# Rotary attention on one NeuronCore: the inverted softmax sums, split in two parts, are spread over the heads by eight 128-row fp32r products instead of sixteen 32-row fp32 ones

## The reference, cut to what matters

```python
q = layer_norm(layernorm(x)); k = v = layer_norm(ctx)       # x: 2 x 2048 x 512, ctx: 2 x 128 x 512
qh, kh = rope(heads(q @ Wq)), rope(heads(k @ Wk))           # 16 heads of 64
vh = heads(v @ Wv)
aw = 30 * tanh((qh . kh) / 8 / 30); aw = where(pad | causal, -inf, aw)
p = softmax(aw, axis=-1)
out = (p . vh, heads side by side) @ Wo
x = x + out
```

## Time and profile before

| | |
|---|---|
| median of 3 runs | 1569.18 us (1568.81 to 1569.34) |
| span of the profiled execution | 1565.3 us |
| median less span | 3.9 us (no separate time is given for the profiled execution) |
| PE busy, DVE busy | 1471.0 us (94%), 1184.2 us (76%) |
| rotary attention's chunks | about 61 to 645 us of the span |
| from one chunk's `recip` to the next | 36.73 us |

### The profile page before, as it was taken

One profiled execution on the slowest core, in us unless ns is written; L12 is line 12 of the kernel. 1 busy time (PEld: TensorE's weight loads), 2 busy tenths in 40 slices (PEclk: granted clock), 3 DMA queues, 4 the chain that ended last, 5 costly groups with the idle time before them and its releaser, 6 DMA issues. The chain is left out here.

```text
span 1565.3 us, 30701 instructions
## 1 busy us (share of the span) xinstructions
PE 1471.0 (94%) x10998; PEld 1078.9 (69%) x11022; DVE 1184.2 (76%) x2306; ACT 881.9 (56%) x2093; POOL 489.1 (31%) x436
## 2 busy tenths in 40 slices
PE   7899999999999999599998998999999977998997
PEld 5677777777777777444443467888888866776885
DVE  5677777886777655478878968888888756787875
ACT  3444444444444443456657838888988865664342
POOL 0122222222222221200002544545545434664333
PEclk9999999999999999799999999999999998999998
DMA  8411111110111101113304810000000007225641
GB/s 308 153 45 44 44 44 44 44 40 8 43 34 34 43 8 75 44 75 148 148 1 178 324 40 3 4 2 2 3 4 3 4 1 269 82 82 182 205 151 60
DMA packets 47808, 118.35 MB, mean 76 GB/s; under 512 B 9422, under 2 KB 15950, under 8 KB 46032
## 3 DMA queue, kind: packets, MB, share of 16 engines
q1 hardware_dynamic: 42016, 100.03, 18.1%
q0 software_dynamic: 5680, 16.85, 2.7%
HBM read 78.89 MB, written 39.80 MB: 76 GB/s over the span
## 5 line engine op out<-in xcount | busy, mean ns | idle before, releaser
L1721 ACT ACTIVATE c_probs<-c_score,c_minus_top 128x128 f32<-128x128 f32 x512 | 183.8, 422 | 2.0 <-DVE c_minus_top L1833 2.0
L1676 POOL TENSOR_TENSOR c_probs<-c_probs,c_recip 128x1024 f32<-128x1024 f32 x64 | 121.7, 1902 | 169.7 <-DVE c_recip L1839 169.7
L689 POOL TENSOR_TENSOR a_attn_lo_parts<-a_attn,a_attn_hi_parts 128x512 fp32r<-128x512 f32 x64 | 80.1, 1285 | 250.2 <-ACT a_attn_hi_parts L747 250.2
L1721 ACT ACTIVATION_READ_ACCUMULATOR c_probs<-c_score,c_minus_top 128x1 f32 x512 | 133.9, 262 | 0.0
L743 ACT COPY a_attn<-a_pv_ps 128x512 f32<-128x512 f32 x64 | 37.0, 578 | 162.7 <-PE a_pv_ps L998 162.6
L425 PE MATMUL a_bank<-a_x_hi_parts,a_wq_hi 128*128 128x256 f32 x512 | 106.8, 290 | 0.3 <-PEq L440 0.3
L2287 ACT CAST d_xT_hi<-d_turn 128x512 fp32r<-128x512 f32 x71 | 41.7, 587 | 110.1 <-PE d_turn L2531 103.1
L425 PE MATMUL a_bank<-a_x_lo_parts,a_wq_hi 128*128 128x256 f32 x512 | 103.0, 283 | 0.0
L425 PE MATMUL a_bank<-a_x_hi_parts,a_wq_lo 128*128 128x256 f32 x512 | 102.8, 282 | 0.0
L966 PE MATMUL a_bank<-a_wo_hi,a_attn_hi_parts 128*128 128x512 f32 x256 | 102.4, 400 | 0.0
L967 PE MATMUL a_bank<-a_wo_lo,a_attn_hi_parts 128*128 128x512 f32 x256 | 101.1, 395 | 0.0
(11 more groups left out here) (310 smaller groups left out, 4276.0 us busy)
## 6 DMA issues: line engine op xcount, KB each, us to landing
hidden<-b_hidden SPq DMA_DIRECT2D x5, 2816.0 KB, 8.1
b_hidden<-hidden SPq DMA_DIRECT2D x5, 2816.0 KB, 11.9
xres<-in_x SPq DMA_DIRECT2D x8, 1024.0 KB, 14.0
d_we<-in_we SPq DMA_DIRECT2D x8, 1024.0 KB, 12.7
xres<-in_w_gate_up SPq DMA_DIRECT2D x7, 1024.0 KB, 5.3
d_got<-rows SPq DMA_DIRECT2D x20, 258.0 KB, 2.9
xres<-rows SPq DMA_DIRECT2D x19, 258.0 KB, 2.9
a_rot<-in_rot SPq DMA_DIRECT2D x16, 256.0 KB, 3.1
```

The source lines that it names most:

```text
L689: nc.gpsimd.tensor_tensor(of_spread(attn_lo, g), of_spread(attn, g), of_spread(attn_hi, g), ALU.subtract).then_inc(attn_lo_ready, 1)
L1676: nc.gpsimd.tensor_tensor(part, part, recip[:, t % 2, heads].unsqueeze(2).to_broadcast([P, HALF, KEYS]), ALU.mult).then_inc(scaled, 1)
L1721: last = nc.scalar.activation(probs[:, t, at, :], score_ps[:, h, g, :], ACT.Exp, bias=minus_top[:, h, g:g + 1], accum_out=total[:, t, at:a ...
```

## The change

The inverted sums are made in three steps on DVE: `reciprocal` into half of the scratch tile `swapped`, a copy of it rounded to fp32r into the other half, and a `scalar_tensor_tensor` that writes rounded * s + full into the fp32r tile `recip`, where s is 0 on the rows with row % 32 < 16 and -1 on the others. So half of the rows hold the rounded value and the other half the rest. Each step waits for the one before. The products of `spread` now use all 128 rows: one product gives the 128 rows of two heads, with a 0/1 matrix that has two ones in each column (rounded part and rest), 4 products a `spread`, 8 a chunk. That matrix (`pick_heads`, 128x1024) is made once by POOL at the start of the second block; TensorE waits for it once, in chunk 0. To make room, `q` holds two units instead of four and its buffer is used in turn, and `x_full` moves from `q` to the place of `x_lo`.

```diff
-        sum_to, pick = sb("sum_to", [P, 32 + UNITS - 1]), sb("pick", [P, UNITS])
+        sum_to, pick = sb("sum_to", [P, 32 + UNITS - 1]), sb("pick", [P, H0 + 1])
...
-        recip = sb("recip", [P, ROPE_CHUNK])
+        recip = sb("recip", [P, ROPE_CHUNK], F32R)
+        recip_full, recip_hi = swapped[:, 0, :], swapped[:, 1, :].bitcast(F32R)
...
-        q = sb("q", [P, BLOCKS, ROPE_CHUNK])
-
-        x_full = q[:, 0:KB, :]
+        q = sb("q", [P, 2, 2, ROPE_CHUNK])
+        pick_heads = sb("pick_heads", [P, H0, DH0], F32R)
+
+        x_full = nc.alloc_sbuf_tensor_at("a_x_full", [P, KB, ROPE_CHUNK], F32, offset=front_offset + 4 * KB * ROPE_CHUNK)
...
+                nc.gpsimd.tensor_copy(pick_heads[:], pick[:, 0:H0].unsqueeze(2).to_broadcast([P, H0, DH0])).then_inc(pick_ready, 1)
                 chunks(pool, body)
...
-                    nc.vector.tensor_tensor(q[:, 2 * g:2 * g + 2, :], src[:], by_angle(0), ALU.mult)
+                    nc.vector.tensor_tensor(q[:, g % 2], src[:], by_angle(0), ALU.mult)
...
                         dve.wait_ge(summed, UNITS * (n + 1))
-                        nc.vector.reciprocal(recip[:], sum_ps[:, 0, :]).then_inc(recip_ready, 1)
+                        ch.step(nc.vector.reciprocal(recip_full, sum_ps[:, 0, :]))
+                        ch.wait()
+                        ch.step(nc.vector.tensor_copy(recip_hi, recip_full))
+                        ch.wait()
+                        nc.vector.scalar_tensor_tensor(recip[:], recip_hi, pick[:, H0:], recip_full, ALU.mult, ALU.add).then_inc(recip_ready, 1)
...
                         if m == 0:
                             pe.wait_ge(recip_ready, n + 1)
+                            if isinstance(n, int) and n == 0:
+                                pe.wait_ge(pick_ready, 1)
                         out = [begin(f"B{2 * m + i}") for i in range(2)]
                         for i in range(2):
-                            for h in range(4):
-                                rows = slice(32 * h, 32 * (h + 1))
-                                last = nc.tensor.matmul(out[h // 2][h % 2 * DH0:(h % 2 + 1) * DH0, i, :], pick[rows, 2 * m + i:2 * m + i + 1].to_broadcast([32, DH0]), recip[rows, :],
-                                                        start=True, stop=True)
+                            for j in range(2):
+                                heads = slice(H0 // UNITS * (2 * m + i) + 2 * j, H0 // UNITS * (2 * m + i) + 2 * j + 2)
+                                last = nc.tensor.matmul(out[j][:, i, :], pick_heads[:, heads, :].rearrange("p h d -> p (h d)"), recip[:], start=True, stop=True)
                         last.then_inc(bank_full, 2)
...
-        "pick": (at[:, None] % 32 == np.arange(UNITS)[None, :]).astype(np.float32),
+        "pick": np.concatenate([(at[:, None] % 16 == np.repeat(np.arange(UNITS), 4)[None, :]) & (at[:, None] // 32 == np.tile(np.arange(4), UNITS)[None, :]),
+                                -1.0 * (at[:, None] % 32 >= 16)], axis=1).astype(np.float32),
```

More of the change, by code:

```diff
@@ L325, in rope_attention_stage @@
         summed, recip_ready = sem("summed"), sem("recip_ready")
-        dve_step = sem("dve_step")
+        dve_step, pick_ready = sem("dve_step"), sem("pick_ready")
         ld_raw, weight_step, piece_ready, stored, ld_last = (sem(x) for x in ("ld_raw", "weight_step", "piece_ready", "stored", "ld_last_x"))
@@ L615, in rope_attention_stage @@
         assert next_offset(nc) <= ahead.top
-        DVE_STEPS = 2 * NT + UNITS - 1
+        DVE_STEPS = 2 * NT + UNITS - 1 + 2
         score_banks = score_ps[:].rearrange("p u h c -> p (u h c)").bitcast(BF16).rearrange("p (i c) -> p i c", i=4)
@@ L810, in rotate_end @@
                         ch.wait()
-                    unit = q[:, 2 * g:2 * g + 2, :]
+                    unit = q[:, g % 2]
                     nc.vector.tensor_tensor(unit, unit, swapped[:], ALU.add).then_inc(q_ready, 1)
@@ L982, in scores @@
                         rows, m = slice(h % 2 * DH0, (h % 2 + 1) * DH0), 2 * p + h // 2
-                        last = nc.tensor.matmul(score_ps[:, p % 2, place(h), :], keysT[rows, m, b * KEYS:(b + 1) * KEYS], q[rows, m, :],
+                        last = nc.tensor.matmul(score_ps[:, p % 2, place(h), :], keysT[rows, m, b * KEYS:(b + 1) * KEYS], q[rows, p % 2, h // 2, :],
                                                 start=True, stop=True)
```

## The result

Over ten runs of each kernel the median is 1560.72 us (1557.83 to 1566.73) after and 1570.85 us (1566.27 to 1573.78) before. The ratio over all these runs is 0.9942, with a 95% interval of 0.9928 to 0.9955: 9.1 us less, between 7.1 and 11.3 (the two medians lie 10.1 us apart). The forecast was 10.4 us less, 1558.8 us, range 1556.0 to 1563.3. The profiled execution has a span of 1558.6 us.

A forecast was written before the change was run, and what follows sets the result against it. TensorE was taken to bound the rotary stage. 15 chunks x 0.70 us less 0.05 us in the last gave 10.4 us saved: 1569.2 - 10.4 = 1558.8 us, range 1556 to 1563.3 us.

The forecast's parts named there:

- What bounds: Rotary stage, chunks 0 to 14: TensorE alone fills the time (544.35 of 550.00 us), so time spared there is kept.
- Removed and added on TensorE: Each spread: 1.02 us of four concurrent groups replaced by four fp32r products in 0.67 us, saving 0.35 us.
- Added on DVE: Before rotating Q0: copy and combination add 0.75 us, at most about 0.95, hidden under 1.14 us idle in chunks 0 to 14.
- What is late next: Around the spreads: slacks of 0.56 us at spread(1), 0.49 at values(n+1, 0), 0.13 at project(Q2); no loss counted.
- Sum: Whole kernel: 15 chunks x 0.70 us saved, 10.5 us, less 0.05 us in the last chunk, 10.4 us in all.
- Last chunk: Inversion uncovered there: spread(0) starts 0.75 us later, the cheaper spreads make up most of it, loss 0.05 us.
- The prediction's rival: Part given back, by late weights, project(Q2) overrun or the clock in 649 to 700 us; gain 3.1 to 8 us, chance 0.12.
- Later stages "shift as a whole": Stages after the rotary one: independent of its clock time, so they move earlier unchanged.
- Start: Beginning of the chunks: POOL makes pick_heads in 14.27 us of idle time, costing nothing or up to 1 us once.

The follow-up runs named there:

- halved products: Changed kernel with each fp32r spread product cut to the 64 rows of its two heads; ratio to the kernel before 0.9923, median 1556.46 us.
- without the split: Changed kernel with the reciprocal writing fp32r directly, rounded once, the rest of each inverted sum left out; 1556.52 us, measured once.
- early sums: Kernel with halved products, in the last chunk sums(3) moved into output(1) and the inversion put ahead of DVE's addition; ratio to before 0.9896, median 1552.48 us.

## Why the prediction was right

- **What bounds.** TensorE is the bound of chunks 0 to 14 and kept what it was spared: the distance fell with the spreads, without a new wait.
- **Removed and added on TensorE.** 0.35 us a spread was forecast, 0.36 and 0.35 measured (1.02 to 0.66 and 0.67). The prices read off `project`, 0.12 us a product with 0.10 and 0.09 at the edges, were right part by part: in the first spread the second product starts 0.22 us behind the first, the next two 0.12 and 0.11, and `values` 0.21 behind the last. The run with halved products lost 0.43 us where 0.44 was expected, but with other parts than assumed, so the prices hold for this shape and aren't shown for that one. The concurrency of the old small products was the point on which the size hung: the fp32 run over 128 rows shows that without the type the change loses 0.90 us a spread. "TensorE: Matmul & The Clock Gate", Part 3, of the Trainium skill speaks for small products on different row groups; the halved products follow it in fp32r, two side by side (starts 0.01 us apart), and are the faster form here: 1.30 us from `scores` to `values` against 1.73.
- **Added on DVE.** 290 ns were estimated for the copy and 290 measured; 425 taken for the combination, 480 measured; 0.84 us with the waits instead of 0.75, all under idle time of 1.14 us, of which 0.29 are left. The run without the split confirms that it costs a chunk nothing, the runs with more copies that the cover ends near 2 us.
- **What is late next.** The list of slacks held: `weigh(0)` lost its wait, `project(Q2)` with 0.13 us to spare wasn't overrun. The slacks of 0.56 us before `spread(1)` and 0.49 us before `values(n+1, 0)` were overrun as soon as the spread got cheaper still.
- **Sum: mis-sized by 0.07 us a chunk.** The term 15 x 0.70 measured 0.63 in one profile and 0.55 (36.73 - 36.18) in the other, since `output` runs 0.08 us a chunk slower in the one and 0.15 in the other. I had set the moved and widened tiles at 0. The wider `pick` alone does this to the kernel before.
- **Last chunk: mis-sized.** 0.05 us were forecast. Without a fall of the clock that is about right: 46.52 before and 45.96 with the 40 wide `pick`, 0.56 less, where 0.70 of chunk 14 less 0.05 and the slower output were due; from the inversion of chunk 15 on it is 10.80 us before and 10.87 with that `pick`, 0.07 lost. In both profiles of the changed kernel the clock fell in this place, and 46.50 and 46.51 us remained, 0.5 us more. The prediction's rival had the clock behind the stage, not in it.
- **Later stages "shift as a whole": only roughly.** +1.3 us stand before the feed-forward stage, where POOL's reduction over partitions starts 5.1 to 7.9 us behind the end of its input in the 14 profiles (6.7, 5.5 and 5.2 in those of before, 7.9 and 7.4 in those of the changed kernel); and +2.0 us in the masked attention, where both profiles of the changed kernel have 368.1 us and the three of before 366.1. Other kernels with the changed spread have 366.0 to 366.1 too (without the split, with halved products, with the 40 wide `pick`) or 368.0 to 368.1 (fp32, copies four and seven times, early sums), and the kernel before with the wider `pick` has 368.3 to 368.6, so it isn't the change as such but how the lower clock level falls on that stage: over its last 40 us the granted clock is 0.91 before (1262 to 1302) and 0.84 after (1255 to 1295). The prediction had put 1 to 2 us for it into the range, at another place.
- **Start.** POOL's copy took 1.04 us in idle time (7.88 us of it were left before its next instruction). Nothing was lost.
- **What of the number is luck.** The forecast of 1558.8 us was 10.4 less than a median of three, 1569.18; over ten runs the kernel before has 1570.85, so 1.7 of the 1.9 us between forecast and measurement are the base. The gain, 9.1 us, lies near what the distances give, 15 x 0.55 to 15 x 0.63 = 8.3 to 9.5 us. Start, last chunk and later stages moved by up to 2 us each in single profiles, in both directions, so the distance of the inversions carries the proof and not the total.

What stays open: why the position of tiles changes the pace of 512 column products, what picks one of several paces in one and the same kernel, and what decides whether the clock falls in the last chunk.

## What to carry to other kernels

Small matmuls that share the array must be counted in groups, by the distance of starts in the timeline; merging them into full-array products won here only together with a cheaper type, and halves that keep the array part of the neighbour were cheaper still. When the bound engine gets cheaper, list the slack of everybody who meets it: the smallest number of that list whose two ends don't move together is where the next saving ends (here 0.49 and 0.56 us, not the 0.13). Work added under idle time is free in the steady loop and bare in the last iteration, so look there for the same chain.

## What the runs showed of the hardware that was not expected

- Moving tiles by 64 bytes in SBUF changed the pace of unchanged matmuls: 0.15 us in the 48 products of 512 columns of a chunk, 0.17 us in the chunk (36.73 to 36.90).
- One kernel's identical loop ran at 36.10 us in one execution and 36.18 in another, each constant to 0.002 us over a loop.
- An fp32 product of 256 columns over the whole array takes two records of 0.24 us on average, 1.92 us for four products, against 0.12 us for an fp32r product.
- The fp32r products with 64 rows start 0.02 us behind the last pair of `scores`, which uses the same part of the array, where a change of part (the spread over 128 rows) starts 0.31 us behind; but the second pair follows 0.30 us behind the first, so part of that is only put off.
